# A Gram product whose second half is made of three fp32r passes

## What is computed

```
# layer 0, x and ctx as [b, n, c]
attn = softmax(einsum('bhni,bhnj->bhij', q, k) * d**-0.5)   # q, k, v are x or ctx times a 128x128 matrix
p2r = (v(ctx) @ attn(q(x), k(ctx))) @ proj_p2r.T
r2p = (v(x) @ attn(q(ctx), k(x))) @ proj_r2p.T
x1  = x + p2r + ctx + r2p
# layer 1, queries and keys from ctx, values from x1
scores = einsum('bhdl,bhel->bhde', Wq ctx + bq, Wk ctx + bk) / sqrt(E)
o   = Wo (softmax(scores) (Wv x1 + bv)) + bo + x1
out = (o - mean(o)) * rsqrt(var(o) + eps) * gn_w + gn_b     # mean and variance over channels and positions
```

## Time and profile before

| | |
|---|---|
| median of 3 runs (range) | 376.43 us (376.25 to 378.23) |
| the profiled execution | 372.62 us, its span 370.8 us |
| mean granted TensorE clock | 0.991 |
| busy: TensorE, VectorE, ScalarE, GpSimd | 341.6, 262.8, 214.1, 214.8 us |
| line 320, Gram matmuls | 512 records, 128.0 us busy |
| fp32r passes of 512 columns, lines 340, 341, 345 | 144.5 us busy |
| line 911, `split_low` | 256 pieces, 178.0 us |

### The profile page before, as it was taken

The page is one execution under the profiler, slowest core; times in us unless marked ns, Lnnn a source line. Parts: engine busy times, 40 slices in busy tenths (PEclk is TensorE's granted clock), DMA queues, the critical chain, the costliest instruction groups (busy, mean ns, idle before and its releaser), DMA issues.

```text
span 370.8 us, 7768 instructions
## 1 busy us (share of the span) xinstructions
PE 341.6 (92%) x2422; PEld 291.4 (79%) x2422; DVE 262.8 (71%) x653; ACT 214.1 (58%) x333; POOL 214.8 (58%) x323
## 2 busy tenths in 40 slices
PE   6887499999999999999999999999999999999772
PEld 3776388888888888888888888888888888888651
DVE  1473276877788686877789686877779687777574
ACT  2455145766665666756666566756566576666312
POOL 0299318476674837576583837576583837677001
PEclk9999899999999999999999999999999999999998
DMA  7653855566656565565647466565746565202022
GB/s 271 233 173 103 287 173 169 177 223 206 215 190 201 201 193 227 177 217 187 245 156 217 177 182 228 192 221 167 259 156 194 204 185 197 113 0 89 26 114 113
DMA packets 30250, 67.29 MB, mean 181 GB/s; under 512 B 2336, under 2 KB 17824, under 8 KB 30240
## 3 DMA queue, kind: packets, MB, share of 16 engines
q1 hardware_dynamic: 30240, 67.17, 54.1%
HBM read 50.39 MB, written 16.78 MB: 181 GB/s over the span
## 4 chain that ended last, share of the span: by engine, by line
PE 84%; DMA 4%; POOL 3%; DVE 3%; ACT 2%; issue 2%; SPq 0%; POOLq 0%
PE gacc L320 30%; PE oacc L340 8%; PE oacc L345 8%; PE oacc L341 8%; PE tpx L297 7%; PE mid L402 6%; PE mid L422 4%; PE mid L364 3%; POOL xy_lo L911 3%; DMA raw<-in_x 3%; PE mid L408 2%; PE mid L367 2%; PE mid L409 2%; PE mid L411 2%; DMA raw<-in_ctx 2%
## 5 line engine op out<-in xcount | busy, mean ns | idle before, releaser
L911 POOL TENSOR_TENSOR xy_lo<-raw,xy_hi 128x256 fp32r<-128x256 f32 x256 | 178.0, 738 | 18.0 <-ACT xy_hi L528 15.7
L320 PE MATMUL gacc<-t 128*128 128x257 f32 x512 | 128.0, 388 | 5.6 <-ACT gram L519 5.5
L320 PEld LDWEIGHTS gacc<-t 128*128 128x128 f32 x512 | 91.2, 190 | 18.4 <-issue 7.1
L899 POOL TENSOR_TENSOR attn<-probs,sinv 32x192 f32<-32x192 f32 x46 | 25.6, 557 | 91.6 <-DVE sinv L779 89.7
L528 ACT ACTIVATE xy_hi<-raw 128x1024 fp32r<-128x1024 f32 x64 | 67.3, 1054 | 1.4 <-DMA raw<-in_ctx 1.4
L654 DVE STREAM_TRANSPOSE t<-y_blocks 128x512 f32<-128x512 f32 x60 | 67.1, 1119 | 0.0
L535 ACT ACTIVATE res<-oacc 128x512 f32<-128x512 f32 x60 | 35.7, 596 | 52.2 <-PE oacc L345 52.2
L665 DVE BATCH_NORM_STATS2 hstat<-res 128x6 f32<-128x512 f32 x60 | 40.7, 678 | 34.7 <-ACT res L535 34.7
L340 PE MATMUL oacc<-xy_hi,pq_hi 128*128 128x512 f32 x124 | 56.0, 452 | 0.7 <-ACT pq_hi L510 0.7
L341 PE MATMUL oacc<-xy_lo,pq_hi 128*128 128x512 f32 x124 | 49.2, 397 | 0.0
L492 ACT ACTIVATE t<-tpx 128x512 f32<-128x512 f32 x64 | 38.0, 593 | 17.0 <-PE tpx L297 16.9
(11 more groups left out here) (98 smaller groups left out, 429.4 us busy)
## 6 DMA issues: line engine op xcount, KB each, us to landing
raw<-in_x SPq DMA_DIRECT2D x32, 512.0 KB, 4.1
raw<-in_ctx SPq DMA_DIRECT2D x32, 512.0 KB, 8.0
out<-res SPq DMA_DIRECT2D x32, 512.0 KB, 8.1
y_blocks<-in_ctx SPq DMA_DIRECT2D x120, 128.0 KB
wt<-in_weights SPq DMA_DIRECT2D x1, 896.0 KB, 8.5
cst<-in_consts SPq DMA_DIRECT2D x1, 147.0 KB, 3.4
quad<-in_quad_rows SPq DMA_DIRECT2D x1, 32.0 KB, 7.0
vec<-in_vectors SPq DMA_DIRECT2D x1, 2.0 KB, 5.9
```

The costliest lines, as they stand in the source:

```text
L320: mm = pe.matmul(gacc[:, 0:2 * C + 1], t[slot][:, c, C:2 * C], t[slot][:, c, :], start=(c == 0), stop=(c == CH - 1))
L911: piece = pool.tensor_tensor(xy_lo[slot][:, s, cols], raw[slot][:, s, cols], xy_hi[slot][:, s, cols].bitcast(f32), ALU.subtract)
```

## The change

Of each batch's Gram product the first four chunks stay as they were, but with a 258th column (a second column of ones) beside them. The second four chunks take three fp32r passes each: high y by [high y, high x, ones] in 258 columns, high y by [low y, low x] in 256, low y by [high y, high x, ones] in 258. The product low by low is left out. The high parts are made by ScalarE: `xt_out` now writes its second half into an fp32r tile `t_hi`, and a new `yt_high` rounds the transposed y, which VectorE puts into a float32 tile `yt`. The low parts `t_lo` are made by two new VectorE operations: `x_low` (PSUM bank `tpx[1]` minus `t_hi`) and `y_low` (`yt` minus `t_hi`). The buffers `t`, `t_hi`, `t_lo` and `yt` are two each, by b, in place of the four of `t`. The core of the diff:

```diff
-        t = [sb(f"t{n}", [C, CH, 2 * C + 1]) for n in range(TB)]
-        gram = sb("gram", [C, 2, 2 * C + 1])
+        t = [sb(f"t{n}", [C, HC, 2 * C + 2]) for n in range(2)]
+        t_hi = [sb(f"t_hi{n}", [C, HC, 2 * C + 2], f32r) for n in range(2)]
+        t_lo = [sb(f"t_lo{n}", [C, HC, 2 * C], f32r) for n in range(2)]
+        yt = [sb(f"yt{n}", [C, HC, C]) for n in range(2)]
+        gram = sb("gram", [C, 2, 2 * C + 2])
...
# TensorE, x_transpose
-                    pe.wait_ge(xt_ready, n - 1)
+                    if i == 0:
+                        pe.wait_ge(xt_ready, n - 1)
+                    else:
+                        pe.wait_ge(xlo_ready, 4 * h + slot)
...
# TensorE, gram_chunks
+                if begin == HC:
+                    pe.wait_ge(xlo_ready, n + 1)
+                    pe.wait_ge(ylo_ready, n + 1)
+                for c in range(begin, min(end, HC)):
+                    mm = pe.matmul(gacc[:, 0:2 * C + 2], t[b][:, c, C:2 * C], t[b][:, c, :],
+                                   start=(c == 0), stop=False)
+                for c in range(max(begin - HC, 0), end - HC):
+                    yhi, ylo = t_hi[b][:, c, C:2 * C], t_lo[b][:, c, C:2 * C]
+                    pe.matmul(gacc[:, 0:2 * C + 2], yhi, t_hi[b][:, c, :], start=False, stop=False)
+                    pe.matmul(gacc[:, 0:2 * C], yhi, t_lo[b][:, c, :], start=False, stop=False,
+                              skip_group_check=True)
+                    mm = pe.matmul(gacc[:, 0:2 * C + 2], ylo, t_hi[b][:, c, :], start=False,
+                                   stop=(c == HC - 1))
...
# ScalarE
+            def yt_high(h, u, b):
+
+                n = 4 * h + 2 * u + b
+                act.wait_ge(yt_ready, 2 * n + 2)
+                act.activation(t_hi[b][:, :, C:2 * C], yt[b][:, :, :], ACT.Copy).then_inc(yhi_ready, 1)
...
# VectorE
+            def x_low(h, u, b):
+
+                n = 4 * h + 2 * u + b
+                dve.wait_ge(xt_ready, 2 * n + 2)
+                dve.tensor_tensor(t_lo[b][:, :, 0:C], tpx[1][:, :, :], t_hi[b][:, :, 0:C].bitcast(f32), ALU.subtract)\
+                    .then_inc(xlo_ready, 1)
+
+            def y_low(h, u, b):
+
+                n = 4 * h + 2 * u + b
+                dve.wait_ge(yhi_ready, n + 1)
+                dve.tensor_tensor(t_lo[b][:, :, C:2 * C], yt[b][:, :, :], t_hi[b][:, :, C:2 * C].bitcast(f32),
+                                  ALU.subtract).then_inc(ylo_ready, 1)
...
# VectorE, step: after shift_scores, and again with b = 1 after partition_moments
+                if front and middle:
+                    x_low(h, u, 0)
+                    y_low(h, u, 0)
...
# ScalarE, step: after xt_out(h, u, 0, 1) and after xt_out(h, u, 1, 1)
+                    yt_high(h, u, 0)
...
+                    yt_high(h, u, 1)
```

More of the change, by code:

```diff
@@ L16 @@
 LAST_DVE_QUADS = 3
-TB = 4
 PIECES = 4
@@ L136, in cross_attention_pair_kernel @@
         yt_ready = sem("yt_ready")
+        yhi_ready = sem("yhi_ready")
+        xlo_ready = sem("xlo_ready")
+        ylo_ready = sem("ylo_ready")
         gram_done = sem("gram_done")
@@ L284, in _ @@
             pe.wait_ge(consts_in, 16)
-            pe.wait_ge(ones_set, TB)
+            pe.wait_ge(ones_set, 4)
             def x_transpose(h, u, b, i):
@@ L310, in gram_chunks @@
             def gram_chunks(h, u, b, begin, end):
[L312 to L321, removed]
+                n = 4 * h + 2 * u + b
+                if begin == 0:
+                    pe.wait_ge(xt_ready, 2 * n + 1)
+                    pe.wait_ge(yt_ready, 2 * n + 1)
+                    if not (isinstance(n, int) and n < 1):
+                        pe.wait_ge(gram_ready, n)
+                if begin == HC:
[11 more added lines that the diff above has]
+                                   stop=(c == HC - 1))
                 if end == CH:
@@ L485, in xt_out @@
             def xt_out(h, u, b, i):
-                slot = 2 * u + b
-                n = 4 * h + slot
+                n = 4 * h + 2 * u + b
                 act.wait_ge(x_transposed, 2 * n + i + 1)
[L490 to L493, removed]
+                if i == 0 and not (isinstance(n, int) and n < 2):
+                    act.wait_ge(gram_done, n - 1)
+                act.activation((t, t_hi)[i][b][:, :, 0:C], tpx[i][:, :, :], ACT.Copy).then_inc(xt_ready, 1)
+            def yt_high(h, u, b):
+                n = 4 * h + 2 * u + b
+                act.wait_ge(yt_ready, 2 * n + 2)
+                act.activation(t_hi[b][:, :, C:2 * C], yt[b][:, :, :], ACT.Copy).then_inc(yhi_ready, 1)
             def u12_out(p):
@@ L518, in gram_out @@
                     act.wait_ge(sk_ready, p)
-                act.activation(gram[:, b, :], gacc[:, 0:2 * C + 1], ACT.Copy).then_inc(gram_ready, 1)
+                act.activation(gram[:, b, :], gacc[:, 0:2 * C + 2], ACT.Copy).then_inc(gram_ready, 1)
             def split_high(h, u, b, s, back):
@@ L610, in _ @@
             dve.memset(attn[:, :, :], 0.0).then_inc(attn_zero, 1)
-            for n in range(TB):
+            for n in range(2):
                 dve.memset(t[n][:, :, 2 * C:], 1.0).then_inc(ones_set, 1)
+                dve.memset(t_hi[n][:, :, 2 * C:].bitcast(f32), 1.0).then_inc(ones_set, 1)
             dve.memset(gate[:, 1:2], 0.0).then_inc(o_out, 2)
@@ L640, in y_first_out @@
                 dve.wait_ge(y_first_done, 2 * b + i + 1)
-                dve.tensor_copy(t[b][:, HC * i:HC * (i + 1), C:2 * C],
+                dve.tensor_copy((t[b][:, :, C:2 * C], yt[b][:, :, :])[i],
                                 y_first[b][i][:, :].rearrange("p (c r) -> p c r", r=C)).then_inc(yt_ready, 1)
@@ L816, in step @@
                             y_first_out(b, i)
+                        x_low(h, u, b)
+                        y_low(h, u, b)
                     prepare()
@@ L845, in step @@
                     partition_moments(p - 2, u)
+                if front and middle:
+                    x_low(h, u, 1)
+                    y_low(h, u, 1)
                 if middle:
```

8 lines of the change are left out of this document (5 added, 3 removed).

## The result

The changed kernel takes **399.37 us** (median of 4 runs, 398.14 to 401.22), the kernel before 376.44: a ratio of **1.061**, 95% interval 1.056 to 1.066. The forecast was 402.5, the range 390 to 414. The profiled execution has a span of 398.3 us. Prologue and tail of one and the same kernel differ by several us, largely with the clock that TensorE is granted there (before, in the executions beside the experiments: those of 371 to 374 us had a mean clock of 0.979 to 0.992, most of them 0.986 or more, and those of 376 us and above 0.970 to 0.982), so I compare steps of the loop, beside medians.

A forecast was written before the change was run, and what follows sets the result against it. TensorE, 92% busy, was taken as the bound, the helpers' ring 0.56 us shorter; the subtractions make the ring 22.84. 24.4 for 13 rings, 1.1 and 0.6 give +26.1 on 376.4: 402.5 us, range 390 to 414.

The forecast's parts named there:

- The ring: Dependency loop through all four engines once a step, waits taken out: 20.40 us before, 22.84 after the change.
- The loss of 1.88 a step: Loop step of 20.96 us becomes the ring's 22.84; over 13 rings 24.4 us more.
- The subtractions: x_low and y_low on VectorE: 0.68 us long, 0.61 to the next start, 1.22 a batch on the ring.
- TensorE's saving of 0.48 a step: Second four chunks: three passes 0.375 us against 0.435 native, 0.06 saved on each of eight chunks a step.
- rival 5: TensorE: a 258-column fp32r pass costs 0.435 us like a native chunk; 7 us more a step, 488 us; chance 0.03.
- The stall before attn: TensorE waits 1.5 to 2 us a step before the attn products, put down to GpSimd's attn.
- Prologue: New operations delay TensorE some 1.4 us in each of two steps; the 4.80 x-transfer wait hides about 3.
- 1.1 for the first step and 0.6 for the tail: Beyond 13 rings: first loop step adds 1.1 us by batch 0; late gram_out in the tail adds 0.6.
- TensorE staying the bound: Rival 1: VectorE does the subtractions in existing waits, so the 7.7 us saving comes in full: 369 us; chance 0.04.
- one pair only: Rival 2: only one batch's subtractions are on the ring: 21.62 us a step, 386 us; chance 0.10.
- GpSimd in the way of `y_low`: Rival 3: both y_low slide into GpSimd's pieces, 2 x 0.43 a step, 11 us more: 414 us; chance 0.06.
- The clock: Rival 4: TensorE's clock falls in the new stall of about 2 us: 409, up to 440 us; chance 0.03.

The follow-up runs named there:

- no_low: Changed kernel without x_low and y_low of both batches, low parts set to zero once: 372.2 us, ratio 0.990 to the kernel before.
- low_b0: Changed kernel with only batch 0's subtractions (after shift_scores), batch 1's low part zero: 385.25 us, ratio 1.028 to the kernel before.
- low_b1: Changed kernel with only batch 1's subtractions (after partition_moments), batch 0's low part zero: 388.27 us, ratio 1.033 to the kernel before.
- moved_x: moved_2 without y_low, the low part of y being zero; both x_low stay on VectorE: 372.6 us, ratio 0.986 to the kernel before.
- native_high: Changed kernel with one native matmul of the rounded high parts per second-four chunk instead of three fp32r passes: 398.18 us, ratio 1.062.
- moved_2: As moved, but y_low of batch 1 stands in VectorE's wait for GpSimd's power, its yt_high after the last out_to_sbuf: 379.13 us, ratio 1.010.
- moved_2_native: moved_2 with one native matmul of the rounded high parts for each of the second four chunks: 386.74 us, ratio 1.032.
- after_again: The changed kernel once more, unaltered, beside the others on the same chip: 400.15 us, ratio 1.061 to the kernel before.
- moved: Changed kernel, full arithmetic, with subtractions and yt_high moved to helpers' waits, and TensorE's transposes and chunks reordered: 377.8 us, ratio 1.007.
- moved_3: As moved_2, but both y_low on GpSimd, before attn and before the power, from the second pair on: 377.75 us, ratio 1.004.
- moved_4: moved_3 with y_low of batch 0 on VectorE behind batch 1's first y transpose, batch 1's on GpSimd after the moments: 383.55 us, ratio 1.024.

## Why the prediction was right, and where it was off

- **The ring.** I put it at 20.40 us before and 22.84 after; the step is 22.74. Segment by segment in the changed kernel: moments to n12 +1.22, softmax shift to row sums 2.82 for 1.66 + 1.22 = 2.88, sk to the shift 4.38 for 4.57, attn 1.82, hand-over 0.14, line 419 and the out half 2.82 for 2.73. So the main term is right, and shown by no_low, low_b0 and low_b1. The segment that was most off is sk to the shift: I took 0.22 and 0.21 as all of VectorE's waiting there; it did the same work in 0.19 less. Other segments came out longer, so that the ring without the new work is 22.74 - 4 x 0.60 = 20.34, and the spare in the step of 20.96 was 0.62 and not 0.56.
- **What I missed.** The forecast took the step as the greater of two numbers, the ring of the helpers and TensorE's work. There is a third, the path told at moved_x, half in TensorE's queue and half in the softmax. It did not show in the changed kernel, where the helpers' ring is longer, but it is why moved_x stops at 20.75. In no_low its two parts are 15.8 and 4.9 of the 20.72, in low_b0 15.83 and 5.88 of the 21.71, and in both line 419 starts 0.14 to 0.15 behind attn in every step; VectorE follows the scores at 0.36 in about half of them, so it is at least close to the bound there.
- **The loss of 1.88 a step** was mis-sized: 1.74, since the step before is 21.00 as a mean and the ring 22.74. 13 steps give 22.6 instead of 24.4.
- **The subtractions** at 0.68 long and 0.60 apart are as priced.
- **TensorE's saving of 0.48 a step** was mis-sized. A pass of 258 columns takes 0.12, as the rows of 512 said (so rival 5, at 0.435, is out), but the first of a group takes 0.20. The trace of before had the like: its out product's first pass, at 108.78, has its successor at 109.09, 0.31 later, where I read 0.23 from the later ones. A group of four chunks therefore takes 1.51 instead of 1.74 and saves 0.23; one of two chunks takes 0.81 (six passes) instead of 0.87 and saves 0.06. A step has one group of four and two of two: 0.35. It is hidden here anyway, as native_high shows. In the order of moved_2 there are two groups of four, 0.46. That moved_2 against moved_2_native gives 0.47 is luck, since it is 0.61 less 0.14. Moved_x should by TensorE's work be 0.46 under the kernel before and is 0.25 under it. Between the scores and line 419 TensorE's own work would be 4.36 in its order (4.79 before, less two chunks, 0.87, plus four transposes, 0.44), but the softmax takes 4.64 there, as told at moved_x: 0.28 lost.
- **The stall before attn** was 1.28, I wrote 1.5 to 2. TensorE lost the rest elsewhere: 0.24 before the pq products, as forecast, and 0.2 before `u_products` for `gram_out`, which I had not listed.
- **Prologue.** I hid 3 us under the wait of 4.80 for an x transfer. TensorE came to that wait 2.7 us later. About half of it hid, 3.40 of the wait being left, and the first loop step starts at 45.41 instead of 44.08; the transfer was issued 1.19 later:

```profile
34.49 1.19 SPq L206 DMA_DIRECT2D raw<-in_x  x1
```
```profile
35.68 1.19 SPq L211 DMA_DIRECT2D raw<-in_x  x1
```

  That is the condition which the prediction named for them to come back. Whether the change made the transfer late I can't show: the loop's first moments operation lies between 60.4 and 64.7 in the thirteen traces, and in the two of the changed kernel at 63.14 and 61.42.
- **From span to median.** I added 3.8 us, the distance of the profiled execution of before from its median. But the profiled execution of before was granted 0.991 as a mean, more than most executions of before beside the experiments (0.970 to 0.982 in those of 376 us and above). The one of the changed kernel, granted 0.985, lies close to its own median. In its tail the passes of the out product stand 0.42 apart (granted clock 0.51, the lower of the two levels), where those of before stand 0.24 apart (1.00):

```profile
383.27 0.63 PE L357 MATMUL oacc<-xy_hi,pq_hi 128*128 128x512 f32 x1
383.69 0.63 PE L358 MATMUL oacc<-xy_lo,pq_hi 128*128 128x512 f32 x1
```
```profile
357.25 0.40 PE L340 MATMUL oacc<-xy_hi,pq_hi 128*128 128x512 f32 x1
357.49 0.40 PE L341 MATMUL oacc<-xy_lo,pq_hi 128*128 128x512 f32 x1
```

  So the profiled spans differ by 27.5 us and the medians by 22.9. The loop gives 22.6 of either. The prediction's 1.1 for the first step and 0.6 for the tail would make it 24.3, but no run shows these two, and that after_again gave 24.3 too is luck, with executions 7 us apart.
- **Rivals.** TensorE staying the bound is out by the step of 22.74, and one pair only by the two half kernels. GpSimd in the way of `y_low` did not happen in the changed kernel, where both `y_low` fall between GpSimd's operations, as the rows had it; it made attn and the power long in moved and moved_2, as moved_x shows, and is seen in the traces of moved_3 and moved_4. The rule that I cited from the Trainium skill, SBUF — State Buffer, section Who interferes with whom, agrees with moved and moved_x: `y_low`, with two SBUF inputs, lengthens attn to 2.29, and `x_low`, with one, leaves it at 1.82. The clock did not fall in the new stalls, which were 1.3 us and not the 2 of the rival: 1.00 through the loop.

## What to carry to other kernels

When one engine is 99% busy and in-order queues pass results round once a step, add up the ring of the others with its waits taken out, and also the paths that run partly in the busy engine's queue and partly outside it: here the first was 0.6 us of 21 short of the bound, and four operations of 0.6 us turned a kernel bound by TensorE into one 6% slower bound by latency. A VectorE that is busy 78% of the time can still have no spare time at the place where the new operation stands. And of two places that are free by VectorE's waits, look at what GpSimd does at that moment if both read two SBUF tensors.

## What the runs showed of the hardware that I had not expected

- Where a VectorE operation with two SBUF inputs and a GpSimd one overlapped, either could be the longer for it: attn 1.83 to 2.29, the power 0.69 to 1.19, `y_low` 0.68 to 1.04, abv_m 0.21 to 0.50, the moments 0.79 to 1.34, the variance pair 0.35 to 0.79. It isn't always both: `y_low` kept 0.67 beside the lengthened attn, and 0.64 beside the lengthened pieces of moved_4. What decides which of the two pays stays open.
- In the Gram groups the first fp32r pass, which stands behind a native float32 matmul, has its successor 0.20 us later, the others 0.12.
- In the two traces of the changed kernel the loop's step agrees to 0.01 us, while what follows the loop differs by 1.1 us, its start by 1.7, and whole executions of this kernel by up to 7 us.
